# A gated delta network: decay differences from rows spread by DMA and subtracted on VectorE, and the last level of the block inverse in two orders

## The reference

```python
def step(state, xs):
    q_t, k_t, v_t, g_t, b_t = xs
    state = state * jnp.exp(g_t)[..., None, None]
    kv = jnp.einsum('bhk,bhkv->bhv', k_t, state)
    delta = (v_t - kv) * b_t[..., None]
    state = state + jnp.einsum('bhk,bhv->bhkv', k_t, delta)
    out = jnp.einsum('bhk,bhkv->bhv', q_t, state)
    return (state, out)
```

## Time and profile before

| | us |
|---|---|
| median of 3 runs | 1398.15 (1395.53 to 1399.49) |
| the profiled execution | 1400.72 |
| its span, first to last instruction | 1398.9 |
| PE busy in the span | 1289.0 (92%) |
| DVE busy | 969.0 (69%) |
| ACT busy | 790.9 (57%) |
| POOL busy | 753.2 (54%) |

### The profile page before, as it was taken

One profiled execution on the slowest core, in us unless ns is written; L12 is line 12 of the kernel. 1 busy time (PEld: TensorE's weight loads), 2 busy tenths in 40 slices (PEclk: granted clock), 3 DMA queues, 4 the chain that ended last, 5 costly groups with the idle time before them and its releaser, 6 DMA issues. The chain is left out here.

```text
span 1398.9 us, 24967 instructions
## 1 busy us (share of the span) xinstructions
PE 1289.0 (92%) x8680; PEld 875.8 (63%) x8680; DVE 969.0 (69%) x1922; ACT 790.9 (57%) x1947; POOL 753.2 (54%) x1245
## 2 busy tenths in 40 slices
PE   6859999999999999999999999898997899499993
PEld 3347767677677676776776767666454566346672
DVE  5848888888888888888888888755222565441554
ACT  3546867677777676777766767654322554210220
POOL 1675886867767868677677686810000000144463
PEclk9869999999999999999999999998998999699997
DMA  2425355474464553744646537462007900122587
GB/s 87 113 74 118 101 146 142 98 183 118 109 170 110 153 134 97 180 114 125 166 111 154 133 95 179 116 201 68 0 1 304 275 1 1 68 72 94 125 187 186
DMA packets 233180, 171.71 MB, mean 123 GB/s; under 512 B 163746, under 2 KB 202998, under 8 KB 230240
## 3 DMA queue, kind: packets, MB, share of 16 engines
q1 hardware_dynamic: 226912, 161.59, 43.6%
q0 software_dynamic: 6144, 8.53, 3.4%
HBM read 104.64 MB, written 65.83 MB: 122 GB/s over the span
## 5 line engine op out<-in xcount | busy, mean ns | idle before, releaser
L723 PE MATMUL psum_banks<-main_hT,gdn_w_in 128*128 128x512 f32 x512 | 255.2, 609 | 7.4 <-DMA gdn_w_in<-in_w_in 4.1
L1227 DVE SCALAR_TENSOR_TENSOR heads_y<-psum_banks,gdn_conv_w,heads_y 128x1021 f32<-128x1021 f32 (+2 forms) x192 | 244.7, 1275 | 21.7 <-ACT heads_y L1033 17.5
L1522 POOL TENSOR_TENSOR heads_XT<-heads_XT,heads_tmp 128x126 f32<-128x126 f32 (+22 forms) x496 | 198.6, 400 | 38.9
L1519 POOL TENSOR_TENSOR heads_tmp<-heads_XT,heads_A 128x126 f32<-128x126 f32 (+22 forms) x496 | 189.6, 382 | 41.5 <-PE psum_banks L902 1.8
L723 PEld LDWEIGHTS psum_banks<-main_hT,gdn_w_in 128*128 128x128 f32 x512 | 93.5, 194 | 62.1 <-issue 52.7
L849 PE MATMUL psum_banks<-heads_w_z,main_hT 128*128 128x256 f32 x512 | 128.8, 384 | 0.0
L871 PE MATMUL psum_banks<-heads_ogT,heads_w_o 128*128 128x512 f32 x240 | 126.4, 609 | 0.2 <-issue 0.2
L849 PEld LDWEIGHTS psum_banks<-heads_w_z,main_hT 128*128 128x128 f32 x512 | 95.2, 191 | 25.2 <-issue 14.4
L1033 ACT ACTIVATE heads_y<-psum_banks,gdn_conv_w 128x1024 f32<-128x1024 f32 x64 | 71.3, 1114 | 69.3 <-PE psum_banks L723 69.0
L1057 ACT ACTIVATE heads_O<-psum_banks,heads_coef 128x128 f32<-128x128 f32 x224 | 69.6, 363 | 70.5 <-PE psum_banks L756 70.3
L1490 POOL TENSOR_TENSOR heads_og<-heads_og,heads_fac 128x512 f32<-128x512 f32 x60 | 61.2, 1041 | 80.1 <-DVE heads_fac L1294 80.1
(11 more groups left out here) (295 smaller groups left out, 3026.4 us busy)
## 6 DMA issues: line engine op xcount, KB each, us to landing
values_by_tokens<-heads_v_s SPq DMA_DIRECT2D x64, 256.0 KB, 4.2
heads_v_s<-values_by_tokens SPq DMA_DIRECT2D x16, 1024.0 KB, 5.1
outputs_by_features<-heads_ogT SPq DMA_DIRECT2D x120, 128.0 KB, 2.4
heads_ogT<-outputs_by_features SPq DMA_DIRECT2D x30, 512.0 KB, 3.8
main_w_gu<-in_w_gu SPq DMA_DIRECT2D x4, 2816.0 KB, 21.0
gdn_w_in<-in_w_in SPq DMA_DIRECT2D x16, 512.0 KB, 4.3
heads_A<-kk_blocks SPq DMA_DIRECT2D x64, 128.0 KB, 2.7
keys_by_tokens<-heads_k_tok SPq DMA_DIRECT2D x64, 128.0 KB, 4.2
```

The costliest lines, as they stand in the source:

```text
L723: ins = pe.matmul(out[:, half * 512:(half + 1) * 512], w_in[:, kd_, j * P:(j + 1) * P], hT[:, kd_, half * 512:(half + 1) * 512], start=kd_ ...
L1227: dve.scalar_tensor_tensor(y[j][:, shift:T], src[:, 0:T - shift], conv_w[:, head, j, t:t + 1], y[j][:, shift:T], ALU.mult, ALU.add).then_i ...
L1519: pool.tensor_tensor(tmp[:, 0:n, 0:m], bc_last(XT[:, 0:n, j], m), bc_mid(A0[:, j, j + 1:BLK], n), ALU.mult).then_inc(solve_step.sem, 1)
L1522: pool.tensor_tensor(XT[:, 0:n, j + 1:BLK], XT[:, 0:n, j + 1:BLK], tmp[:, 0:n, 0:m], ALU.add).then_inc(solve_step.sem, 1)
```

## The change

Decays: the running sums are stored once, without their negatives, and one DMA for each head spreads its 16 rows of 128 over all 128 partitions, straight into `Dm` (1 MB), which now has two buffers. `decay0` to `decay3` are 16 DVE instructions on SBUF: subtract the own G as a scalar, take the minimum with `limit`. PE has no decay products any more. Level 64: chunks 0 to 3 keep the order; for chunks 4 to 7 the product with the lower-right inverse comes first (`y7b`), so that one block `y7a` and `y7b`, and one block `u7a` and `u7b`, hold two products beside each other in different rows of the array. The order lists of all engines are new (one line of each is shown).

```diff
 PE_PLAN = """
-z0/2:0 tx0 z0/2:1 o0 p0/-1:0 p0/-1:1 su0 p1/-1:0 p1/-1:1 ks1 z1/1:0 qs1 z1/1:1 tx1 norm_q/2 z2/3:0 z2/3:1 o1 su1
+p0/-1:0 tx0 z0/0:0 z0/0:1 p0/-1:1 o0 su0 p1/-1:0 p1/-1:1 z1/2:0 norm_q/0 ks1 qs1 z1/2:1 z2/1:0 tx1 z2/1:1 o1 su1
...
 SP_PLAN = """
-values_out inverse_out values_in products_out inverse_in products_in outputs_out0 outputs_in0 w_z outputs_out1
-outputs_in1 kt_out kt_in w_in w_o gates
+kt_out values_out gates inverse_out values_in products_out inverse_in products_in outputs_out0 outputs_in0 kt_in
+outputs_out1 w_in outputs_in1 w_z w_o
 """.split()
 POOL_PLAN = """
-pow q_root norm0 norm1 norm2 scale norm3 solve
+q_root pow norm0 norm1 norm2 scale norm3 solve
...
-    if name in ("w_in", "gates"):
+    if name == "w_in":
         return h + 2 < HK
+    if name == "gates":
+        return 0 < h < HK - 1
...
-    Dm = a.sb("Dm", [P, IT, P])
+    Dm = [a.sb(f"Dm{i}", [P, IT, P]) for i in range(2)]
...
             def gate_rows(h):
-                for sign, rows in enumerate([row_to, row_from]):
-                    src = cum_rows[sign, IT * h:IT * (h + 1)].rearrange("(g s) t -> g s t", g=4)
-                    sp.dma_start(rows[h % 2][sign:P:32], src).then_inc(s_rows[h % 2], 16)
+                src = cum_rows[IT * h:IT * (h + 1)].rearrange("i t -> (i t)").unsqueeze(0)
+                sp.dma_start(flat(Dm[h % 2][:]), src.to_broadcast([P, IT * P])).then_inc(s_rows[h % 2], 16)
...
                 elif name == "gates":
-                    b = bank_of(h, "decay3")
-                    sp.wait_ge(full[b].sem, full[b].done(h, "decay3"))
-                    gate_rows(h + 2)
+                    sp.wait_ge(uf_ready.sem, uf_ready.base(h))
+                    gate_rows(h + 1)
...
-                elif name == "decay0":
-                    for s in range(4):
-                        for g in range(4):
-                            r, out = slice(32 * g, 32 * g + 2), bank[bank_of(h, f"decay{g}")]
-                            ins = pe.matmul(out[:, s], row_from[par][r, s], row_to[par][r, s], start=True, stop=True)
...
+                elif name == "y7a":
+                    ba, bb = bank_of(h, "y7a"), bank_of(h, "y7b")
+                    half = C // 2
+                    for j in range(half):
+                        c, d = j, half + j
+                        ia = pe.matmul(bank[ba][64:128, j], kneg[par][0:64, c, 64:128], Xh[0:64, c:IT:C], start=True, stop=True)
+                        ib = pe.matmul(bank[bb][0:64, j], kneg[par][64:128, d, 0:64], Uf[par][64:128, d:IT:C, 64:128], start=True, stop=True)
...
+                elif name == "u7a":
+                    ba, bb = bank_of(h, "u7a"), bank_of(h, "u7b")
+                    right = flat(kneg[par][0:64, 0:4])
+                    for i in range(IT // 2):
+                        e, j = i // 4, i % 4
+                        at, mine = slice(i * 64, (i + 1) * 64), j * HD + e
+                        ia = pe.matmul(flat(bank[ba][:])[0:64, at], Y7[64:128, mine], Uf[par][64:128, e * C + j, 64:128], start=True, stop=True)
+                        ib = pe.matmul(flat(bank[bb][:])[0:64, at], Xh[0:64, e * C + 4 + j], right[:, mine * 64:(mine + 1) * 64],
+                                       start=True, stop=True)
...
+                elif name == "y7b":
+                    act.wait_ge(full[bank_of(h, "y7a")].sem, full[bank_of(h, "y7a")].done(h, "y7a"))
+                    act.activation(flat(kneg[par][0:64, 0:4]), flat(bank[b][:])[0:64], ACT.Copy).then_inc(free[b].sem, 1)
...
+                if name.startswith("decay"):
+                    if u == 0:
+                        dve.wait_ge(s_rows[par], 16 * (h // 2 + 1))
+                    for i in range(4 * u, 4 * u + 4):
+                        ins = dve.scalar_tensor_tensor(Dm[par][:, i], Dm[par][:, i], coef[:, G_, h, i:i + 1], limit[:], ALU.subtract, ALU.min)
+                    ins.then_inc(decay_ready.sem, 1)
+                    return
...
-                elif name.startswith("decay"):
-                    dve.wait_ge(full[b].sem, full[b].done(h, name))
-                    dve.tensor_tensor(Dm[:, 4 * u:4 * u + 4], bank[b][:], bc_mid(limit[:], 4), ALU.min).then_inc(free[b].sem, 1)
```

More of the change, by code:

```diff
@@ L208 @@
+p2/-1:0 p2/-1:1 ks2 p3/-1:0 qs2 tx2 p3/-1:1 o2 su2 kk0/2 kk1/1 ks3 qs3 z3/2:0 tx3 z3/2:1 o3 su3 p4/-1:0 ks4 p4/-1:1
+qs4 tx4 p5/-1:0 o4 su4 p5/-1:1 y6a/2 y6b/0 attn0/3 ks5 qs5 u6a/2 u6b/0 tx5 attn1/1 o5 su5 p6/-1:0 p6/-1:1 p7/-1:0
+y7a/2 y7b/0 ks6 p7/-1:1 qs6 out0/2:0 tx6 out0/2:1 o6 su6 u7a/0 u7b/1 out1/3:0 ks7 out2/0:0 qs7 tx7 out2/0:1 o7
+out3/2:0 out1/3:1 out3/2:1
 """
 PE_FIRST = """
-p0/-1:0 p0/-1:1 p1/-1:0 norm_q/2 p1/-1:1 p2/-1:0 decay0/0 decay1/1 decay2/3 decay3/2 p2/-1:1 p3/-1:0 attn1/1 p3/-1:1
@@ L212 @@
-p4/-1:0 kk0/2 p4/-1:1 p5/-1:0 p5/-1:1 p6/-1:0 kk1/2 p6/-1:1 p7/-1:0 attn0/2 p7/-1:1 y6a/3 y6b/2 u6a/3 u6b/0 y7_0/2
-y7_1/2 u7_0/3 u7_1/0
+p0/-1:0 p0/-1:1 p1/-1:0 p1/-1:1 p2/-1:0 p2/-1:1 p3/-1:0 norm_q/3 p3/-1:1 p4/-1:0 kk0/1 p4/-1:1 p5/-1:0 p5/-1:1 p6/-1:0
+p6/-1:1 kk1/0 attn1/3 p7/-1:0 attn0/0 p7/-1:1 y6a/2 y6b/3 u6a/0 u6b/1 y7a/0 y7b/2 u7a/1 u7b/2
 """
 PE_SECOND = """
-p0/-1:0 z0/1:0 p0/-1:1 out0/2:0 tx0 p1/-1:0 z0/1:1 o0 su0 p1/-1:1 ks1 qs1 norm_q/0 z1/1:0 tx1 z2/3:0 z1/1:1 out2/1:0
-o1 su1 z2/3:1 p2/-1:0 decay0/2 decay1/0 decay2/3 decay3/1 out2/1:1 ks2 qs2 out3/2:0 tx2 p2/-1:1 p3/-1:0 o2 su2 kk0/0
@@ L219 @@
-out0/2:1 p3/-1:1 ks3 qs3 kk1/3 tx3 o3 su3 attn0/3 ks4 p4/-1:0 p4/-1:1 qs4 p5/-1:0 tx4 z3/3:0 p5/-1:1 o4 su4 y6a/2
-y6b/1 ks5 z3/3:1 qs5 tx5 attn1/0 u6a/1 u6b/2 o5 out1/0:0 su5 p6/-1:0 ks6 p6/-1:1 qs6 tx6 p7/-1:0 y7_0/2 out1/0:1 o6
-p7/-1:1 su6 y7_1/2 u7_0/0 out3/2:1 ks7 qs7 tx7 u7_1/1 o7
+z0/0:0 p0/-1:0 out2/0:0 p0/-1:1 p1/-1:0 tx0 p1/-1:1 z0/0:1 o0 su0 z2/1:0 out0/0:0 ks1 z1/2:0 qs1 tx1 norm_q/0 o1
+z2/1:1 su1 z1/2:1 ks2 qs2 tx2 p2/-1:0 p2/-1:1 o2 p3/-1:0 p3/-1:1 out2/0:1 su2 kk0/3 ks3 kk1/2 qs3 tx3 z3/3:0 o3
@@ L222 @@
+out3/2:0 su3 ks4 p4/-1:0 qs4 tx4 p4/-1:1 o4 su4 out0/0:1 out1/0:0 p5/-1:0 ks5 qs5 p5/-1:1 tx5 o5 y6a/0 y6b/1 su5
+out3/2:1 z3/3:1 ks6 qs6 attn1/0 tx6 u6a/2 u6b/1 out1/0:1 o6 su6 p6/-1:0 p6/-1:1 p7/-1:0 p7/-1:1 ks7 y7a/1 y7b/2 qs7
+tx7 attn0/3 o7 u7a/0 u7b/2
 """
@@ L790, in product_waits @@
                     pe.wait_ge(act_ready.sem, act_ready.done(h, "sq"))
-                elif name == "decay0":
-                    pe.wait_ge(s_rows[par], 32 * (h // 2 + 1))
-                    for g in range(1, 4):
-                        more = free[bank_of(h, f"decay{g}")]
-                        wait(pe, more, more.ahead(h, f"decay{g}"))
                 elif name.startswith("flip"):
@@ L814, in product_waits @@
                     wait(pe, free[bank_of(h, "u6b")], free[bank_of(h, "u6b")].ahead(h, "u6b"))
-                elif name == "y7_0":
+                elif name == "y7a":
                     pe.wait_ge(x10_ready.sem, x10_ready.done(h, "it"))
                     pe.wait_ge(xh_ready.sem, xh_ready.end(h))
-                elif name == "y7_1":
                     pe.wait_ge(free[bank_of(h, "u6b")].sem, free[bank_of(h, "u6b")].done(h, "u6b"))
-                    wait(pe, free[bank_of(h, "u7_0")], free[bank_of(h, "u7_0")].ahead(h, "u7_0"))
-                    pe.wait_ge(free[bank_of(h, "y7_0")].sem, free[bank_of(h, "y7_0")].done(h, "y7_0"))
-                elif name == "u7_1":
-                    pe.wait_ge(free[bank_of(h, "y7_1")].sem, free[bank_of(h, "y7_1")].done(h, "y7_1"))
-                if name not in ("y6b", "u6b", "u7_0", "decay1", "decay2", "decay3"):
+                    wait(pe, free[bank_of(h, "y7b")], free[bank_of(h, "y7b")].ahead(h, "y7b"))
+                elif name == "u7a":
+                    for done in ("y7a", "y7b"):
+                        pe.wait_ge(free[bank_of(h, done)].sem, free[bank_of(h, done)].done(h, done))
+                    wait(pe, free[bank_of(h, "u7b")], free[bank_of(h, "u7b")].ahead(h, "u7b"))
+                if name not in ("y6b", "u6b", "y7b", "u7b"):
                     wait(pe, free[b], free[b].ahead(h, name))
```

123 lines of the change are left out of this document (47 added, 76 removed).

## The result

| | before | changed |
|---|---|---|
| median, 4 runs each | 1398.82 us | 1462.0 us (1455.63 to 1462.6) |
| ratio | | 1.0446, 95% interval 1.0412 to 1.048 |
| profiled execution, its span | 1400.72, 1398.9 | 1455.63, 1453.8 |

The kernel became 63 us slower. The forecast was 1379 with a range to 1405: wrong in its sign.

What follows compares the result with a forecast made beforehand. PE, busy without gaps, was taken to bound the loop at 56.07 us a step. Saving 2.58 less 1.2 of stall, 1.4 in 14 steps, gave 1400.72 - 19.6 + 1 = 1382 profiled, 1379 against the shown runs; range 1353 to 1405.

Steps and rivals of the forecast that it cites:

- PE's side: PE's work per step: decays gone and level 64 in two blocks save 2.58 us, leaving a floor of 53.5.
- DVE's side: DVE's 16 new decay instructions per step: 0.27 us each, 4.3 in all, plus 2.4 of waits for POOL.
- The stall that should come of it: PE waiting for state updates delayed by DVE and POOL excluding each other: 1.2 us a step, bounds 0 to 2.6.
- The slower rival: POOL's powers shut DVE out during `decay3`: 4.5 us of waiting, a step of 58.0, 1427 in all; 18%.
- the spread delays the inverse: 1 MB spread ahead of the solved blocks' store: turn waits 2 to 3 us, the 2.58 are spent, 1398; 16%.
- Fourteen equal steps: Head loop: steps 1 to 14 counted as full ones, each saving 1.4 us, 19.6 in all.
- 14 x 1.4 less 1: Whole program: 1.4 us saved in each of 14 steps, against a net 1 us added in step 0.

Runs made afterwards that it cites:

- e2_front: The changed kernel with the 1 MB spread issued earlier, between the keys' store and the values' store; 1383.3 us, 0.9898 of the kernel before.
- e3_one: e2_front with only the first of four instructions of each decay group executed from head 1 on (decays wrong); 1366.9 us, 0.9778 of the kernel before.
- e4_dummy: The kernel before plus an unread 1 MB broadcast to spare DRAM ahead of the solved blocks' store; 1454.8 us, 1.0421 of the kernel before.

## Why the prediction was wrong, step by step

**PE's side was close.** Decays off PE and two level-64 blocks were to save 2.58 us and leave 53.5; PE's work is 53.8, 2.2 less than before. The blocks in e2_front:

```profile
354.66 2.74 PE L719 MATMUL psum_banks<-main_hT,gdn_w_in 128*128 128x512 f32 x6
...
357.33 0.32 PE L886 MATMUL psum_banks<-heads_Xh,heads_kneg 64*64 64x128 f32 x1
...
358.35 0.70 PE L741 MATMUL psum_banks<-heads_S,heads_kT 128*128 128x256 f32 x2
...
362.78 0.60 PE L761 MATMUL psum_banks<-heads_Dt,heads_k_tok 128*128 128x256 f32 x2
...
363.31 0.27 PE L896 MATMUL psum_banks<-heads_Uf,heads_Xh 64*64 64x64 f32 x1
...
364.39 1.13 PE L847 MATMUL psum_banks<-heads_ogT,heads_w_o 128*128 128x512 f32 x2
...
365.35 0.59 PE L741 MATMUL psum_banks<-heads_S,heads_kT 128*128 128x256 f32 x2
```

The first block costs 358.35 - 357.33 = 1.02, with 0.09 ahead (357.33 - 354.66 - 3 x 0.86) and 0.1 behind, 1.21 as forecast. The second costs 364.39 - 363.31 = 1.08, with 0.10 ahead and 0.10 behind (365.35 - 364.39 - 0.86), 1.28 against 1.26: products that write the same partitions from different row halves do overlap.

**DVE's side was close.** A group takes 1.13 us undisturbed, 0.28 each where 0.27 was forecast, and 1.70 to 1.82 beside POOL's elimination. By the profile's page all 256 take 93.3 us, 5.8 a head, against 4.3 + 2.4 = 6.7 forecast. The half rate that the Trainium skill ("Vector Engine (DVE) Microarchitecture Reference", "Points that are easy to get wrong") gives for this form would by estimate make a group 4 x 0.40 = 1.6; the trace of this case denies it. The stall that should come of it was put at 1.2 us of PE a step. PE is idle for 0.3 in all (e2_front), and the step falls by 0.2 to 0.6 without the decays (e3_one).

**The powers don't hold DVE.** The fourth group ran from 354.55 for its usual 1.13 us, across this row of POOL:

```profile
354.72 1.68 POOL L1526 TENSOR_TENSOR heads_q_root<-heads_q_norm,heads_powers 128x8 f32<-128x8 f32 x1 [5.41 <-DVE heads_q_norm L1331]
```

The slower rival, 18% at 1427, got the sign and not the cause. The lock of the Trainium skill ("SBUF — State Buffer", "Terms") agrees with the trace for POOL's elimination and not for this power.

**The step that failed: the spread delays the inverse.** It stood there as a rival, with 16%, "the turn waits 2 to 3 us" and "the 2.58 are spent: 1398". It was the case, but larger than the rival said. The store was to land 5.1 us later; it is issued 1.6 us later in the step and lands after 3.1 us more, 4.7 together. But the spread also held SP itself: the issue of the values' load took 4.31 us, and the blocks' load behind it left 2.4 us later. So the turn waits 5.0, and PE, which now gets there sooner, 3.9. Nor did the sum know a price for the clock; it is 1.8 us a step (55.6 busy against 53.8). 3.9 + 1.8 less the 2.2 saved gives 3.5 of the 3.6 us a step. Against the rival stood that the store had 2 us of slack and that POOL set when it starts. The slack was real and too small for a megabyte, and where the store starts says nothing of what runs beside it. The 1 MB was priced by its own landing time (5.1 us) for step 0 and at nothing for its neighbours in the loop's main sum.

**Fourteen equal steps** was wrong too: step 1 has a list of its own and took 52.54 us before. In e2_front, 13 steps give 13 x 1.97 = 25.6 us; step 1 costs 4.4 and step 15 2.9 more than before, up to the first copy 1.8, and 4.1 come back behind the loop: 20.7, where 14 x 1.4 less 1 = 19 was forecast. These are the two profiled executions, the one above and the other below its median; the medians on one chip are only 14.5 us apart (1397.9 and 1383.3). With the spread in the free place the number, 1379, would have held (1383, within its own range of 1366 to 1392), partly by luck: less was saved on PE, less was lost by DVE in the steady steps, and steps 1 and 15, which the sum left out or took for full ones, cost what the others gave.

## What to carry to other kernels

Price a new transfer by what it does to the transfers behind it, in landing time and in the queue's issue time, and look for a pause of the queue (here 6 us in which SP waited for DVE) before it is put ahead of a store that someone's next step waits for. A stall of a full PE can cost more than its length, because the clock can fall behind it (here 1.8 us on 3.9); a wait that was hidden before is not hidden when the engine that asks has become faster.

## What the runs showed of the hardware

- PE behind a gap: the granted clock was 0.50 behind a stand of 4.4 us and 1.00 again 6 us after its end (4 to 7 us in twelve steps), which cost 1.8 us a step on the mean; useless products in the gap gave 1.3 of it back. In e4_dummy gaps of 1 to 2.4 us did it in some steps and not in others.
- A 1 MB broadcast ahead of other transfers on the queue: the issue of one later DMA took 4.31 us instead of 0.34 (3.5 to 4.8 in 14 steps, and 3.3 to 4.4 in e4_dummy), a 1 MB load landed after 9.0 instead of 5.1 us, a store after 7.4 instead of 4.3. With 64 KB in its place the store landed after 3.3 us.
- DVE's four `SCALAR_TENSOR_TENSOR` of 128 columns from SBUF: 1.13 us, 1.70 and 1.82 beside POOL's products of SBUF tiles, 1.13 beside a POOL power of 1.68 us.
